# A state-space scan with experts on one core: GpSimd's waits, seven filler products, and GpSimd making each sixth drive product

## The chip, the core and the metric

The kernel runs on one core of a Trainium2 chip, in one launch. The time is the device time of that core in microseconds. TensorE (PE) multiplies matrices into PSUM; VectorE (DVE), ScalarE (ACT) and GpSimd (POOL) compute elementwise; SyncE (SP) issues most transfers. Each engine executes its own instructions in their order and waits on semaphores.

## The reference, cut to what matters

```
tokens = concat of three Hilbert patch embeddings of x, fused; with txt: 4 sequences of 384 tokens, 192 channels
xz = x @ in_proj_w.T;  x_branch, z = split(xz)
u  = silu(causal_conv4(x_branch));  dt = softplus(u @ dt_w.T + dt_b)
Bv = u @ B_w.T;  Cv = u @ C_w.T
for each of 16 states s, along the tokens t:
    h[t] = exp(dt[t] * A[s]) * h[t-1] + dt[t] * Bv[t, s] * u[t]      # decay * state + drive
    y[t] += h[t] * Cv[t, s]
y = ((y + D * u) * silu(z)) @ out_w.T;  then add and layer norm
router: top 2 of 8 experts per token;  expert = gelu(x @ Wi.T) @ Wo.T;  weighted sum
```

## The kernel before, in words

The tokens are cut into three chunks of 128. Channels lie on the partitions: four sequences of 128 channels and the 64 other channels of two pairs of them make six segments of 128 tokens, so a tile of the scan is 128 x 768, and 128 x 780 with two lead columns for each segment (one that clears the state, one that brings in the carry of the chunk before). The scan phase is one loop of 48 steps, `at` = 16 n + s: chunk n and state s. Each engine has this loop written out, with its own order.

In a step TensorE spreads the row of B over the partitions into a PSUM tile (`spread_b`, L815 to L818; two tiles, `wide(0)` and `wide(1)`, by turns). VectorE multiplies it in place with dt times u (the drive product, L1496), and then scans, with the decay from SBUF and the drive from PSUM (L1501), into one of two `states` tiles. ScalarE makes the decays ahead (`decay_of`, three SBUF tiles, L1225 and L1226) and brings in carries (`bring_carry`, L1233). GpSimd copies the last column of each segment as the carry for the next chunk (L574, steps 0 to 31) and multiplies the state with the row of C (L579) into one of two tiles. TensorE adds these up in PSUM (`sum_states`, L834 and L836), two steps behind. SyncE stores the rows of C to memory (`store_c`) and broadcasts one for each step (`broadcast_c`, L490 to L493, three transfers, a ring of three tiles), and from step 16 loads pieces of the experts' weights between them. VectorE waits before a scan for GpSimd's product of two steps ago.

Other work is inserted between the steps. On VectorE, after the scans of steps 3 and 4 the statistics and the normalisation of the last run of tokens (L1383, into `xn`), after 7 its convolution (L1422, L1426), after 11 the split of B in three bf16 parts (L1435 to L1444), after 13 softplus (L1454 to L1460). In the second and third chunk, after s = 1 the output product of the chunk before (L1505), after s = 7 the residual (L1513), after s = 8 the new rows of h (L1522), after s = 10 the router's rows (L1383, into `xf`), after s = 15 the two largest. GpSimd adds a shift to h (L566) before its waits of steps 1, 5 and 9. TensorE and ScalarE have their parts at other steps. Filler products keep TensorE busy in some places (`keep_warm` L773, `filler` L893).

Before the scan the patches are gathered by GpSimd's transfers (L552), transposed on TensorE (`patch_transposes`, L654), embedded (L660) and fused (L680); ScalarE copies between these. After the scan come the routing, and the loop over 31 tiles of expert rows.

## Time and profile before

| what | us |
|---|---|
| median of 3 runs | 461.56 (461.09 to 464.18) |
| the profiled execution | 460.29 |
| its span in the profile | 458.5 |
| VectorE's first scan starts | 74.2 |
| VectorE's last scan starts | 247.9 |
| mean granted clock of TensorE | 0.905 of 2.4 GHz |

The profile shows one execution. Its time is 1.8 us more than the span, which goes from the first to the last instruction; the median of the runs lies 1.3 us above the profiled execution. A row of the timeline has the start, the duration, the engine, the line, the output and the inputs, how many instructions are merged, and in brackets the idle time before them with what ended it. A float32 matmul shows as two records.

### The profile page before, as it was taken

Reading aid. Unit: us, or ns where it says so; the run is one execution under the profiler, and the core shown is the slowest. Engines: PE = TensorE matmul, PEld = TensorE weight load, DVE = VectorE, ACT = ScalarE, POOL = GpSimd, SP = SyncE. Lnnn points to the kernel's source line nnn. Section 1 sums busy time; section 2 is a strip of 40 time slices with the busy share of each in tenths; the row PEclk is TensorE's granted clock in tenths of the full one; section 3 lists DMA queues with packets and bytes.
Section 4 is the critical chain, followed back from the end, with each engine's and each line's share of the span. In section 5 each row is a group of like instructions: output and inputs, shape, how many; then the busy total and the mean of one; then the engine's idle time right before and its main releaser. Section 6 shows DMA issues by size and latency. Waiting matters only on the chain.

```text
span 458.5 us, 6697 instructions
## 1 busy us (share of the span) xinstructions
PE 383.5 (84%) x2283; PEld 285.0 (62%) x2283; DVE 294.9 (64%) x478; ACT 193.4 (42%) x459; POOL 224.9 (49%) x195
## 2 busy tenths in 40 slices
PE   5896997788758977879678875989999999999980
PEld 4453754454334643536344663979999999999970
DVE  4524379999999999999998638444343434344410
ACT  1555476637714465434642021024444444444430
POOL 6778723644526643656245003145656565656431
PEclk9997898979967996999779959599999999999996
DMA  6200012432424644766554730322323323333323
GB/s 183 60 9 4 7 31 92 125 92 59 127 70 150 172 155 115 214 188 190 133 144 114 310 113 38 104 59 43 48 54 46 54 44 56 47 53 46 43 27 112
DMA packets 33383, 42.76 MB, mean 93 GB/s; under 512 B 8302, under 2 KB 23391, under 8 KB 32783
## 3 DMA queue, kind: packets, MB, share of 16 engines
q1 hardware_dynamic: 26030, 34.76, 25.8%
q0 software_dynamic: 7328, 7.71, 10.9%
q8 instruction: 12, 0.20, 0.2%
q14 instruction: 13, 0.10, 0.1%
HBM read 36.55 MB, written 7.08 MB: 95 GB/s over the span
## 4 chain that ended last, share of the span: by engine, by line
PE 46%; issue 18%; POOL 17%; DVE 12%; DMA 3%; ACT 2%; POOLq 0%; SPq 0%; DVEq 0%; ACTq 0%
PE ps L1020 14%; PE ps L1003 9%; POOL w_all L579 9%; POOL w_all L552 6%; PE ps L1009 6%; DVE w_all L1501 4%; PE ps L834 3%; PE ps L979 2%; DVE ps L1496 2%; PE ps L773 2%; PE ps L993 2%; PE ps L836 1%; DVE y_cm L1426 1%; POOL carry L574 1%; DVE y_cm L1454 1%
## 5 line engine op out<-in xcount | busy, mean ns | idle before, releaser
L579 POOL TENSOR_TENSOR w_all<-w_all 128x768 f32<-128x768 f32 x48 | 81.3, 1693 | 29.4 <-DVE w_all L1501 24.1
L1501 DVE TENSOR_TENSOR_SCAN w_all<-decay,ps 128x780 f32<-128x780 f32 x48 | 85.4, 1779 | 1.6
L610 POOL DMA_INDIRECT sum_dram<-u_cm,tok_row x31 | 50.2, 1618 | 60.8 <-ACT u_cm L1329 58.2
L834 PE MATMUL ps<-w_all,cst 128*128 128x512 f32 x96 | 60.5, 716 | 7.8 <-POOL w_all L579 7.5
L552 POOL DMA_INDIRECT w_all<-in_pix,gidx x42 | 45.1, 1073 | 14.9 <-issue 12.5
L1314 ACT ACTIVATE u_cm<-ps,x_cm 128x128 f32<-128x128 f32 x96 | 26.5, 376 | 54.5 <-PE ps L1009 54.5
L1496 DVE TENSOR_TENSOR ps<-dtu_cm,ps 128x768 f32<-128x768 f32 x48 | 45.5, 947 | 1.2 <-PE ps L818 0.6
L574 POOL COPY carry<-w_all 128x6 f32<-128x6 f32 x32 | 6.7, 209 | 69.7 <-DVE w_all L1501 69.7
L1225 ACT ACTIVATE decay<-dt_cm,a_neg 128x512 f32<-128x512 f32 x48 | 34.2, 712 | 15.4 <-DVE dt_cm L1458 9.8
L595 POOL DMA_INDIRECT dt_cm<-x_dram,tok_in x31 | 31.2, 1005 | 19.3 <-DVE gate_s L1666 10.1
L773 PE MATMUL ps<-cst 128*128 128x256 f32 x114 | 34.5, 461 | 5.2 <-DMA cst<-in_cst 5.2
L1679 DVE COPY x_cm<-w_all 128x1154 f32 x16 | 12.2, 762 | 40.0 <-PE ps L1020 40.0
L836 PEld LDWEIGHTS ps<-w_all,cst 128*128 128x128 f32 x96 | 20.6, 215 | 27.8 <-issue 27.8
L1314 ACT ACTIVATE z_cm<-ps,y_cm 128x128 f32<-128x128 f32 x90 | 24.8, 375 | 27.0 <-PE ps L1009 27.0
L1020 PE MATMUL ps<-x_cm,u_cm 128*128 128x192 f32 x192 | 35.5, 333 | 0.0
L1679 DVE COPY y_cm<-w_all 128x1154 f32 x15 | 11.5, 766 | 35.9 <-PE ps L1020 35.9
L773 PEld LDWEIGHTS ps<-cst 128*128 128x128 f32 x114 | 26.0, 237 | 12.2 <-DMA cst<-in_cst 5.2
L1020 PE MATMUL ps<-y_cm,z_cm 128*128 128x192 f32 x180 | 33.4, 334 | 0.0
L815 PE MATMUL ps<-b_parts,pick 128*128 128x256 bf16 x48 | 14.0, 291 | 21.9 <-DVE w_all L1501 21.9
L1020 PEld LDWEIGHTS ps<-x_cm,u_cm 128*128 128x128 f32 x192 | 31.0, 189 | 1.8
L836 PE MATMUL ps<-w_all,cst 128*128 128x256 f32 x96 | 31.3, 411 | 0.0
L834 PEld LDWEIGHTS ps<-w_all,cst 128*128 128x128 f32 x96 | 17.7, 213 | 20.2 <-POOL w_all L579 15.8
(222 smaller groups left out, 722.5 us busy)
## 6 DMA issues: line engine op xcount, KB each, us to landing
w_all<-c_dram SPq DMA_DIRECT2D x48, 256.0 KB, 3.4
w_all<-c_dram SPq DMA_DIRECT2D x96, 64.0 KB, 3.5
w_all<-in_w_all SPq DMA_DIRECT2D x16, 289.0 KB, 3.9
w_all<-in_w_all SPq DMA_DIRECT2D x4, 1156.0 KB, 6.3
x_dram<-x_cm SPq DMA_DIRECT2D x3, 384.0 KB, 3.7
sum_dram<-h_tok SPq DMA_DIRECT2D x3, 384.0 KB, 3.9
out<-sum_dram SPq DMA_DIRECT2D x4, 288.0 KB, 3.6
w_all<-in_pix,gidx POOLq DMA_INDIRECT x42, 2.4
```

What stands on the lines that cost most here:

```text
L552: pool.indirect_dma_start(dst, None, d[table], bass.IndirectOffsetOnAxis(ap=gidx[:, col:col + 1].bitcast(U32), axis=0)).then_inc(signal, 16)
L579: nc.gpsimd.tensor_tensor(segments(hcs[at % 2]), inner(states[at % 2]), segments(c_sb[at % RING]), ALU.mult).then_inc(hc_rdy, 1)
L610: pool.indirect_dma_start(sum_dram, bass.IndirectOffsetOnAxis(ap=tok_row[:, i:i + 1].bitcast(U32), axis=0), y_out[:, i % 2, :], None, comp ...
L773: nc.tensor.matmul(ps[:, bank, 0:256], ident, cst[:, 0:256], start=True, stop=True)
L834: nc.tensor.matmul(sums[:, 0:4 * P], ident, hcs[at % 2][:, 0:4 * P], start=False, stop=at % S == S - 1, skip_group_check=True)
L836: nc.tensor.matmul(sums[:, 4 * P:6 * P], ident, hcs[at % 2][:, 4 * P:6 * P], start=False, stop=at % S == S - 1, skip_group_check=True).the ...
L1003: nc.tensor.matmul(ps[:, 2 + 2 * p + f // 3, P * (f % 3):P * (f % 3) + P], w[:, W_UA + P * f:W_UA + P * f + P], xe[:, p, 0:P], start=(f % ...
L1020: mm = nc.tensor.matmul(ps[:, 6 + p, 0:C], hid[p][:, P * f:P * f + P], w_now[p][:, W_DN + C * f:W_DN + C * f + C], start=(f == 0), stop=(f ...
L1225: nc.scalar.activation(o[:, 0:NB, :], chunk(dt3, n)[:, 0:NB, :], ACT.Exp, scale=a_neg[:, 0, s:s + 1])
L1314: ins = nc.scalar.activation(hid[p][:, P * f:P * f + P], ps[:, 2 + 2 * p + f // 3, P * (f % 3):P * (f % 3) + P], ACT.Gelu, bias=w_now[p][: ...
L1496: v.tensor_tensor(inner(wide(p)), chunk(dtu3, n), inner(wide(p)), ALU.mult).then_inc(driven, 1)
L1501: v.tensor_tensor_scan(states[p], decay[:, at % RING, :], wide(p), 0.0, ALU.mult, ALU.add).then_inc(scanned, 1)
```

## The change

It has three parts.

- GpSimd waits, before its product of steps 4, 7, 11, 13 (first chunk) and s = 8 and 10 (other chunks), until the work inserted on VectorE after that scan is done (`inserted_work`).
- TensorE makes seven more filler products ahead of the first patch transposes.
- GpSimd makes the drive product of the steps 5, 11, 17, ..., 47, three steps ahead, from a row of B that SyncE broadcasts into a new SBUF tile `b_wide_sb`. It writes the drive into the third decay tile, and ScalarE writes the decay of these steps into the PSUM tile that the drive would have had. TensorE spreads no B in these steps. The rows of B are stored to memory beside those of C. The carry copies go from GpSimd to ScalarE (`save_carry`), and VectorE's scan waits for them. After such a step ScalarE clears the carry's column where the tiles have changed roles.

```
...
+        b_wide_sb = sb("b_wide_sb", [P, 6 * P])
...
-        WARM = {"input weights": 10, "coarse levels": 2, "fine patches": 4, "normed rows": 7, "convolution": 2,
+        WARM = {"input weights": 10, "coarse levels": 2, "fine patches": 4, "patches": 7, "normed rows": 7, "convolution": 2,
...
+
+        def by_pool(at):
+
+            return at % 6 == 5
+
+        def pool_drives(at):
+            return (at + 1) // 6
+
+        def vector_drives(at):
+            return at + 1 - pool_drives(at)
...
-            def store_c(n):
+            def store_bc(n):
...
-                                     packed(bc_rows, n, 2)[64 * half + 3 * S:64 * half + 4 * S, :, a - lo:b - lo])\
-                            .then_inc(c_stored, 16)
+                                     packed(bc_rows, n, 2)[64 * half + 2 * S:64 * half + 4 * S, :, a - lo:b - lo])\
+                            .then_inc(bc_stored, 16)
+
...
             def broadcast_c(at):
 
                 r = at % RING
                 if at >= RING:
                     sp.wait_ge(hc_rdy, at - RING + 1)
-                sp.dma_start(c_sb[r][:, 0:4 * P], c_dram[at:at + 1, :].to_broadcast([P, 4 * P])).then_inc(c_ready[r], 16)
-                for half in range(2):
-                    sp.dma_start(c_sb[r][64 * half:64 * half + 64, 4 * P:6 * P],
-                                 c_dram[at:at + 1, 2 * P * half:2 * P * half + 2 * P].to_broadcast([64, 2 * P]))\
-                        .then_inc(c_ready[r], 16)
+                broadcast_row(c_sb[r], 2 * S * (at // S) + S + at % S, c_ready[r])
+
+            def broadcast_b(at):
+
+                if at >= 6:
+                    sp.wait_ge(pool_driven, pool_drives(at - 6))
+                broadcast_row(b_wide_sb, 2 * S * (at // S) + at % S, b_ready)
...
             for at in range(RING):
                 broadcast_c(at)
+            broadcast_b(5)
             piece = 0
             for at in range(RING, STEPS):
                 if at == S - 3:
-                    store_c(2)
-                if at == S:
-                    sp.wait_ge(c_stored, 16 * 8)
+                    store_bc(2)
                 broadcast_c(at)
+                if at == S - 2:
+                    sp.wait_ge(bc_stored, 16 * 8)
+                if by_pool(at - RING) and at - RING + 6 < STEPS:
+                    broadcast_b(at - RING + 6)
...
+            def inserted_work(n, s):
+
+                if n == 0:
+                    if s == 4:
+                        pool.wait_ge(xn_ready, 3)
+                    elif s == 7:
+                        pool.wait_ge(conv_step, 8 * 3)
+                    elif s == 11:
+                        pool.wait_ge(split_step, 5 * 3)
+                    elif s == 13:
+                        pool.wait_ge(dtu_rdy, 3)
+                elif s == 8:
+                    pool.wait_ge(h_new, n)
+                elif s == 10:
+                    pool.wait_ge(xf_rdy, n)
+
+            def pool_drive(at):
+
+                n = at // S
+                pool.wait_ge(dtu_rdy, min(n + 2, 3))
+                pool.wait_ge(b_ready, 48 * pool_drives(at))
+                pool.wait_ge(scanned, at - RING + 1)
+                nc.gpsimd.tensor_tensor(inner(decay[:, RING - 1, :]), chunk(dtu3, n), segments(b_wide_sb), ALU.mult)\
+                    .then_inc(pool_driven, 1)
+
             for at in range(STEPS):
                 if at in (1, 5, 9):
                     add_shift(at // 4)
                 pool.wait_ge(scanned, at + 1)
-                if at < STEPS - S:
-                    nc.gpsimd.tensor_copy(carry[:, at % S, :].rearrange("p (q o) -> p q o", o=1),
-                                          segments(states[at % 2])[:, :, SEG - 1:SEG]).then_inc(carry_saved, 1)
+                inserted_work(at // S, at % S)
                 pool.wait_ge(c_ready[at % RING], 48 * (at // RING + 1))
                 if at >= 2:
                     pool.wait_ge(summed, at - 1)
                 nc.gpsimd.tensor_tensor(segments(hcs[at % 2]), inner(states[at % 2]), segments(c_sb[at % RING]),
                                         ALU.mult).then_inc(hc_rdy, 1)
+                if by_pool(at + RING):
+                    pool_drive(at + RING)
...
             coarse_rows()
             keep_warm(WARM["fine patches"], 0)
             interpolated(0)
+            keep_warm(WARM["patches"], 7)
             patch_transposes(0)
             keep_warm(1, 7)
             fine_level(0)
...
             def spread_b(at):
 
                 n, s, p = at // S, at % S, at % 2
+                if by_pool(at):
+                    return
                 if at >= 2:
                     pe.wait_ge(scanned, at - 1)
                 else:
...
             def decay_of(at):
                 n, s = at // S, at % S
-                if s == 0:
+                if s == 0 or s == 1:
                     act.wait_ge(dt_rdy, min(n + 2, 3))
-                if at >= RING:
-                    act.wait_ge(scanned, at - RING + 1)
-                o = inner(decay[:, at % RING, :])
+                if by_pool(at):
+                    act.wait_ge(scanned, at - 1)
+                    o = inner(wide(at % 2))
+                    if n:
+                        lead = segments(wide(at % 2))
+                        nc.scalar.activation(lead[:, :, 1:2], lead[:, :, 0:1], ACT.Copy)
+                else:
+                    if at >= RING:
+                        act.wait_ge(scanned, at - RING + 1)
+                    o = inner(decay[:, at % RING, :])
+                    if n and by_pool(at - RING):
+                        lead = segments(decay[:, at % RING, :])
+                        nc.scalar.activation(lead[:, :, 1:2], lead[:, :, 0:1], ACT.Copy)
                 nc.scalar.activation(o[:, 0:NB, :], chunk(dt3, n)[:, 0:NB, :], ACT.Exp, scale=a_neg[:, 0, s:s + 1])
                 nc.scalar.activation(o[:, NB:6, :], chunk(dt3, n)[:, NB:6, :], ACT.Exp, scale=a_neg[:, 1, s:s + 1])\
                     .then_inc(decay_rdy, 1)
 
+            def save_carry(at):
+                act.wait_ge(scanned, at + 1)
+                nc.scalar.activation(carry[:, at % S, :].rearrange("p (q o) -> p q o", o=1),
+                                     segments(states[at % 2])[:, :, SEG - 1:SEG], ACT.Copy).then_inc(carry_saved, 1)
+
             def bring_carry(at):
 
                 act.wait_ge(carry_saved, at - S + 1)
-                act.wait_ge(b_wide, at + 1)
-                nc.scalar.activation(segments(wide(at % 2))[:, :, 1:2],
+                if by_pool(at):
+                    act.wait_ge(scanned, at - RING + 1)
+                    lead = segments(decay[:, RING - 1, :])
+                else:
+                    act.wait_ge(b_wide, vector_drives(at))
+                    lead = segments(wide(at % 2))
+                nc.scalar.activation(lead[:, :, 1:2],
                                      carry[:, at % S, :].rearrange("p (q o) -> p q o", o=1), ACT.Copy).then_inc(carry_set, 1)
...
             patches_transposed(1)
             for at in range(STEPS):
                 n, s = at // S, at % S
+                if by_pool(at + 1):
+                    decay_of(at + 1)
+                if 0 <= at - 1 < STEPS - S:
+                    save_carry(at - 1)
                 if S <= at + 1 < STEPS:
                     bring_carry(at + 1)
-                if at + 2 < STEPS:
+                if at + 2 < STEPS and not by_pool(at + 2):
                     decay_of(at + 2)
                 if n == 0:
                     if s == 0:
...
                 n, p = at // S, at % 2
                 if at % S == 0:
                     dve.wait_ge(dtu_rdy, min(n + 2, 3))
-                dve.wait_ge(b_wide, at + 1)
                 if n:
                     dve.wait_ge(carry_set, at - S + 1)
-                v.tensor_tensor(inner(wide(p)), chunk(dtu3, n), inner(wide(p)), ALU.mult).then_inc(driven, 1)
-                dve.wait_ge(driven, at + 1)
+                if by_pool(at):
+                    dve.wait_ge(pool_driven, pool_drives(at))
+                    fade, drive = wide(p), decay[:, RING - 1, :]
+                else:
+                    dve.wait_ge(b_wide, vector_drives(at))
+                    v.tensor_tensor(inner(wide(p)), chunk(dtu3, n), inner(wide(p)), ALU.mult).then_inc(driven, 1)
+                    dve.wait_ge(driven, vector_drives(at))
+                    fade, drive = decay[:, at % RING, :], wide(p)
                 dve.wait_ge(decay_rdy, at + 1)
                 if at >= 2:
                     dve.wait_ge(hc_rdy, at - 1)
-                v.tensor_tensor_scan(states[p], decay[:, at % RING, :], wide(p), 0.0, ALU.mult, ALU.add).then_inc(scanned, 1)
+                    if at - 2 < STEPS - S:
+                        dve.wait_ge(carry_saved, at - 1)
+                v.tensor_tensor_scan(states[p], fade, drive, 0.0, ALU.mult, ALU.add).then_inc(scanned, 1)
```

The rows of C and B take the place of `c_dram` in `bc_dram`; semaphores and the waits on them are renamed accordingly.

GpSimd, first chunk, products of steps 2 to 4. Before:

```order
L574 COPY carry<-w_all 128x6 [waits scanned]
L579 TENSOR_TENSOR w_all<-w_all 128x768 [waits summed,c_ready2]
L574 COPY carry<-w_all 128x6 [waits scanned]
L579 TENSOR_TENSOR w_all<-w_all 128x768 [waits summed,c_ready0]
L574 COPY carry<-w_all 128x6 [waits scanned]
L579 TENSOR_TENSOR w_all<-w_all 128x768 [waits summed,c_ready1]
L566 TENSOR_TENSOR h_tok<-h_tok,ln_gb 128x768 [waits xn_ready]
```

Now:

```order
L627 TENSOR_TENSOR w_all<-w_all 128x768 [waits summed,c_ready2,scanned]
L616 TENSOR_TENSOR decay<-dtu_cm,b_wide_sb 128x6x128 [waits scanned,b_ready,dtu_ready]
L627 TENSOR_TENSOR w_all<-w_all 128x768 [waits summed,c_ready0,scanned]
L627 TENSOR_TENSOR w_all<-w_all 128x768 [waits c_ready1,summed,xn_ready,scanned]
L591 TENSOR_TENSOR h_tok<-h_tok,ln_gb 128x768 [waits xn_ready]
```

The carry copies are gone, the drive for step 5 stands behind the product of step 2, and the product of step 4 waits for the normalised rows.

VectorE, steps 16 to 18. Before:

```order
L1496 TENSOR_TENSOR ps<-dtu_cm,ps 128x6x128 [waits carry_set,b_wide,dtu_ready]
L1501 SCALAR_TENSOR_TENSOR w_all<-decay,ps 128x780 [waits hc_rdy,decay_rdy,driven]
L1496 TENSOR_TENSOR ps<-dtu_cm,ps 128x6x128 [waits carry_set,b_wide]
L1501 SCALAR_TENSOR_TENSOR w_all<-decay,ps 128x780 [waits hc_rdy,decay_rdy,driven]
L1505 TENSOR_TENSOR y_cm<-ps,z_cm 128x6x128 [waits summed]
L1496 TENSOR_TENSOR ps<-dtu_cm,ps 128x6x128 [waits carry_set,b_wide]
```

Now:

```order
L1577 TENSOR_TENSOR ps<-dtu_cm,ps 128x6x128 [waits b_wide,carry_set,dtu_ready]
L1585 SCALAR_TENSOR_TENSOR w_all<-decay,ps 128x780 [waits hc_rdy,carry_saved,decay_rdy,driven]
L1585 SCALAR_TENSOR_TENSOR w_all<-ps,decay 128x780 [waits hc_rdy,decay_rdy,carry_saved,pool_driven,carry_set]
L1589 TENSOR_TENSOR y_cm<-ps,z_cm 128x6x128 [waits summed]
L1577 TENSOR_TENSOR ps<-dtu_cm,ps 128x6x128 [waits b_wide,carry_set]
```

The product of step 17 is gone, and its scan has the inputs the other way round.

## Rows read from the trace of the kernel before

**Rows 1.** The page's costliest groups: busy us, mean ns | idle before, its releaser.
```profile
L1501 DVE TENSOR_TENSOR_SCAN w_all<-decay,ps 128x780 f32<-128x780 f32 x48 | 85.4, 1779 | 1.6
...
L574 POOL COPY carry<-w_all 128x6 f32<-128x6 f32 x32 | 6.7, 209 | 69.7 <-DVE w_all L1501 69.7
```

**Rows 2.** VectorE's timeline in a plain step: start us, duration us, line, instruction.
```profile
152.10 0.94 DVE L1496 TENSOR_TENSOR ps<-dtu_cm,ps 128x768 f32<-128x768 f32 x1
...
153.07 1.78 DVE L1501 TENSOR_TENSOR_SCAN w_all<-decay,ps 128x780 f32<-128x780 f32 x1
...
154.77 0.94 DVE L1496 TENSOR_TENSOR ps<-dtu_cm,ps 128x768 f32<-128x768 f32 x1
```

**Rows 3.** GpSimd's timeline.
```profile
90.72 1.81 POOL L566 TENSOR_TENSOR h_tok<-h_tok,ln_gb 128x768 f32<-128x768 f32 x1
...
163.08 1.68 POOL L579 TENSOR_TENSOR w_all<-w_all 128x768 f32<-128x768 f32 x1
```

**Rows 4.** VectorE's timeline outside the scan.
```profile
50.56 1.32 DVE L1383 TENSOR_SCALAR xn<-h_tok,mv,rstd 128x192 f32<-128x192 f32 x4 [0.28 <-DVE rstd L1379]
...
56.81 2.33 DVE L1426 SCALAR_TENSOR_TENSOR y_cm<-x_cm,chan,y_cm 128x512 f32<-128x512 f32 x3
...
64.62 0.48 DVE L1437 SCALAR_TENSOR_TENSOR w_all<-b_parts,cst,w_all 128x256 f32<-128x256 bf16 x1
...
68.05 3.08 DVE L1454 SCALAR_TENSOR_TENSOR y_cm<-w_all,y_cm 128x768 f32<-128x768 f32 x3
...
260.60 1.40 DVE L1522 SCALAR_TENSOR_TENSOR h_tok<-w_all,rstd,h_tok 128x192 f32<-128x192 f32 x4
```

**Rows 5.** VectorE's timeline, the inserted work of the scan.
```profile
88.86 4.09 DVE L1383 TENSOR_SCALAR xn<-h_tok,mv,rstd 128x192 f32<-128x192 f32 x4
...
102.32 3.67 DVE L1426 SCALAR_TENSOR_TENSOR y_cm<-x_cm,chan,y_cm 128x524 f32<-128x524 f32 x3
...
118.76 1.96 DVE L1437 SCALAR_TENSOR_TENSOR w_all<-b_parts,cst,w_all 128x262 f32<-128x262 bf16 x1
...
128.25 4.58 DVE L1454 SCALAR_TENSOR_TENSOR y_cm<-w_all,y_cm 128x786 f32<-128x786 f32 x3
...
168.67 2.83 DVE L1522 SCALAR_TENSOR_TENSOR h_tok<-w_all,rstd,h_tok 128x192 f32<-128x192 f32 x4
...
178.67 2.62 DVE L1383 TENSOR_SCALAR x_cm<-h_tok,mv,rstd 128x192 f32<-128x192 f32 x4
```

**Rows 6.** One window: us; busy PE, PEld, DVE, ACT, POOL; clock; DMA share, GB/s.
```profile
40.50:48.00 7.50, 7.48 (x19) 4.74 (x20) 2.91 (x4) 4.09 (x7) 5.98 (x6) 0.50 0.07 4
```

**Rows 7.** TensorE's timeline, the patch chain.
```profile
40.52 1.05 PE L654 MATMUL ps<-cst,w_all 128*48 128x128 f32 x4 [3.68 <-ACT w_all L1073]
...
42.35 1.97 PE L660 MATMUL ps<-w_all 48*64 48x512 f32 x2
...
45.26 2.77 PE L680 MATMUL ps<-w_all 65*128 65x192 f32 x8
```

**Rows 8.** TensorE's timeline at either clock: sum of states, then B's spreading.
```profile
139.49 2.08 PE L834 MATMUL ps<-w_all,cst 128*128 128x512 f32 x2 [0.23 <-POOL w_all L579]
...
142.21 0.40 PE L815 MATMUL ps<-b_parts,pick 128*128 128x256 bf16 x1
...
157.53 1.13 PE L834 MATMUL ps<-w_all,cst 128*128 128x512 f32 x2
...
158.49 0.59 PE L836 MATMUL ps<-w_all,cst 128*128 128x256 f32 x2
...
158.92 0.27 PE L815 MATMUL ps<-b_parts,pick 128*128 128x256 bf16 x1
```

**Rows 9.** Rows of C: issues with us to landing (page), and SyncE's timeline.
```profile
w_all<-c_dram SPq DMA_DIRECT2D x96, 64.0 KB, 3.5
...
162.48 1.08 SPq L493 DMA_DIRECT2D w_all<-c_dram  x2
```

**Rows 10.** VectorE's timeline beside GpSimd's product at 163.08.
```profile
164.36 1.39 DVE L1513 SCALAR_TENSOR_TENSOR w_all<-ps,mv,ln_gb 128x192 f32<-128x192 f32 x4
```

More of the change, by code:

```diff
@@ L319, in build @@
         bc_copied = sem("bc_copied")
-        c_stored = sem("c_stored")
+        bc_stored = sem("bc_stored")
         split_step = sem("split_step")
@@ L337, in build @@
         driven = sem("driven")
+        b_ready = sem("b_ready")
+        pool_driven = sem("pool_driven")
         scanned = sem("scanned")
@@ L480, in store_c, with broadcast_row @@
                     for half in range(2):
-                        sp.dma_start(c_dram.rearrange("(j s) (b t) -> j s b t", j=NJ, b=NB)
+                        sp.dma_start(bc_dram.rearrange("(j s) (b t) -> j s b t", j=NJ, b=NB)
                                      [j, :, 2 * half:2 * half + 2, a - P * j:b - P * j],
-                                     packed(bc_rows, n, 2)[64 * half + 3 * S:64 * half + 4 * S, :, a - lo:b - lo])\
-                            .then_inc(c_stored, 16)
+                                     packed(bc_rows, n, 2)[64 * half + 2 * S:64 * half + 4 * S, :, a - lo:b - lo])\
+                            .then_inc(bc_stored, 16)
+            def broadcast_row(dst, row, signal):
+                sp.dma_start(dst[:, 0:4 * P], bc_dram[row:row + 1, :].to_broadcast([P, 4 * P])).then_inc(signal, 16)
+                for half in range(2):
+                    sp.dma_start(dst[64 * half:64 * half + 64, 4 * P:6 * P],
+                                 bc_dram[row:row + 1, 2 * P * half:2 * P * half + 2 * P].to_broadcast([64, 2 * P]))\
+                        .then_inc(signal, 16)
             def broadcast_c(at):
@@ L506, in send_rows @@
                                  xf[:, NB * j:NB * j + NB, src:C]).then_inc(x_sent, 16)
-            store_c(0)
-            store_c(1)
-            sp.wait_ge(c_stored, 16 * 4)
+            store_bc(0)
+            store_bc(1)
+            sp.wait_ge(bc_stored, 16 * 4)
             for at in range(RING):
                 broadcast_c(at)
+            broadcast_b(5)
             piece = 0
```

4 lines of the change are left out of this document (2 added, 2 removed).

## The prediction

> **What bounds the kernel now.** I read the page first. Its busy shares are averages over stages and name no bound; its costliest groups do [rows 1]: before its 48 scans VectorE was idle for 1.6 us in total, so from 74.2 to 249.7 us, where the scan steps run, VectorE is the bound. From 299 us on TensorE runs the expert tiles back to back, as the chain of waits tells, and the change touches nothing there. In a plain step its product starts at 152.10, its scan at 153.07, its next product 1.70 later [rows 2]: a period of 2.67 us, of which 0.97 is the product. GpSimd's product takes 1.68 us of that [rows 3], and then it waits for the next scan.
>
> The second thing to see is that some VectorE instructions inserted between steps are far longer than the same work elsewhere. Before and after the scan, when GpSimd has no elementwise work, they take the times of [rows 4]; inside it those of [rows 5]. Each long one overlaps a GpSimd product: the four normalisations at 88.86 take 4.09 us instead of 1.32, and GpSimd's addition of the shift ends at 92.53, 0.4 us before them [rows 3]. They read both operands from SBUF, or write SBUF from SBUF. The scan and its product, with one operand in PSUM, keep 1.78 and 0.94 us beside GpSimd.
>
> The third: TensorE idles 3.68 us before 40.52 and then runs its patch chain at a granted clock of 0.50, which is 1.2 GHz, from 40.5 to 48 [rows 6, 7].
>
> **The warming products.** They fill 36.84 to 40.52, an idle gap on TensorE. From 40.52 three pieces of its work stand on the path, each waited for by ScalarE and then VectorE: 1.05, 1.97 and 2.77 us at 1.2 GHz. That level costs twice the other: the same sum of states takes 2.72 us from its start to the next matmul at 1.2 GHz and 1.39 at 2.4 [rows 8]. So 5.79 us become 2.9: **2.9 us gained**. Seven products at 2.4 GHz take 7 x 0.43 = 3.0 us, which nearly fills the gap; 0.43 is the distance from 158.49 to 158.92, a matmul of the same shape [rows 8]. Lower bound of the gain: nothing, if the clock falls anyway. What is late next is VectorE's chain from 48.06, which simply starts sooner; the seven products behind it halve too and stay under cover.
>
> **GpSimd's waits.** Six places, priced by [rows 5] minus [rows 4], scaled to 131 columns instead of 128 where needed: normalisation of the input 4.09 - 1.32 = 2.77; convolution 3.67 - 2.38 = 1.29; splitting B 1.96 - 0.49 = 1.47; softplus 4.58 - 3.15 = 1.43; new rows of h 2.83 - 1.40 = 1.43, twice; router's rows 2.62 - 1.32 = 1.30, twice. **12.4 us gained.** The wait delays GpSimd's product of that step to the end of the inserted work. Behind it on GpSimd stand the next products, and VectorE's scan two steps on waits for it; that scan starts 0.97 + 1.70 + 0.97 = 3.6 us later, and the product takes 1.68, so nothing appears there. Two exceptions below.
>
> **The eight drive products.** VectorE drops eight of 0.97 us: **7.8 us gained**. GpSimd adds eight of 1.68 us in slots where it is idle: with its six products and one drive it has 11.8 us of work in 15.1. It makes the drive three steps ahead, right after its product of step D-3. Taking the end of scan D-3 as 0: product 0.05 to 1.75, drive to 3.45, product D-2 to 5.2 instead of 4.4, while scan D may start at 5.35. It fits, by 0.15 us. The 32 carry copies (6.7 us in all on GpSimd [rows 1]) go to ScalarE; their cover is its idle time in every step, and if that went, each would cost 0.2 us. The decay that goes to PSUM is the same two activations; a small copy that clears the carry's place comes to 11 of them, beside the same idle time. The eight extra broadcasts cost SP some 1.5 us each, as each of C's does (1.08 for its last two pieces, after the first). A C broadcast has 5.4 us or more from its release to its use, and needs 0.9 to issue its last piece and 3.5 for it to land [rows 9]. The rows of B double the size of eight small stores to memory, which nobody waits for while VectorE is held. Their second wait moves from step 16 to 14 on SP; the store was issued a step before, and behind it stands only the row for step 15, used two steps later.
>
> **What comes back.**
> - GpSimd, step 8: the delayed product 7, product 8, drive 11 and the addition of the shift (1.8 us, as at 90.72 [rows 3]) queue before product 9. Scan 11 waits for that: 1.6 us (0 to 1.8).
> - TensorE's order: behind the late product D-2 stand its sum (1.4) and only then the spreading of B for step D+1 (some 0.5), and from step 16 on the carry on ScalarE (0.2 and the signals). That ends at 7.6 or so where VectorE wants it at 7.15. Where inserted work follows (D = 5, 11, 17, 23, 41) it is covered; at D = 29 and 35 I put 0.3 and 0.7. Bounds 0 and 8 x 0.7.
> - ScalarE: the decay of step 5 goes before its table load at 85.67, and the decay of step 29 behind the router's copies: 0.3 + 0.5.
> - Softplus into the second chunk: product 13 now starts only after softplus, so TensorE idles some 6 us and then sums at 1.2 GHz (2.72 each); the first output product needs three sums in a row. 1.5 us (0 to 3).
> Together 4.9.
>
> **A page's rule against it.** The four instructions at 164.36 [rows 10] have their first operand in PSUM and their second in SBUF; the first of them runs beside a GpSimd product that ends at 164.76 [rows 3], and the four take 1.39 us. Four of the same size with GpSimd idle take 1.40 [rows 4]. So I take the new scans, decay from PSUM and drive from SBUF, at 1.78. The Trainium skill, page "SBUF — State Buffer", section "Who interferes with whom", says that a VectorE instruction with two SBUF inputs contends with GpSimd's reads because its second input comes through the shared read interface. Read for the second input alone, that would make the eight new scans and GpSimd block each other, and the sum 451 (the first rival); the same section also says that an instruction with at most one SBUF input does not contend, which is what this row shows.
>
> **Sum.** 2.9 + 12.4 + 7.8 = 23.1 us gained, 4.9 given back: 18.2. The profiled execution took 460.29 us (span 458.5): 442.1. The median of the runs, 461.56, stands 1.27 above it, so **443.4 us**. Its own range is 440 (little given back) to 447 (clock and order at their bounds).
>
> **Rivals.**
> - *The shared operand path (0.10).* The new scans and GpSimd's products exclude each other. Scan D starts at 5.35, product D-1 would start at 5.41 and now at 7.15; scan D+1 waits 0.3 us more, the spreading for D+2 some 0.6. About 1 us a step: 8 us, 451. For: the instructions of [rows 5]. Against: [rows 10].
> - *The waits only move the stall (0.07).* The late products surface in later scans: 443.4 + 12.4 = 455.8. Against: 3.6 us of room for 1.68.
> - *The warming does not hold the clock (0.10).* 446.3. For: the clock fell inside an idle gap; against: the gap is filled.
> - *SP's queue (0.05).* B's broadcasts push C's: up to 8 x 1.5 = 12 us, 455.4. For: C's rows already take 4.4 of the 5.4 us that a shorter step leaves [rows 9]. Against: B's broadcast stands behind C's of the same step, and the next row of C has a step more.
> - *TensorE becomes the bound at 1.2 GHz (0.03), slower than before.* A step there takes it 2.72 (sum) + 0.86 (filler, twice 0.43) + 0.4 (spreading, the row at 142.21 alone) = 4.0 us [rows 8], 1.3 more than the period. The waits and the eight missing spreadings lengthen its idle times, and if the low level held for more than 18.2 / 1.3 = 14 steps beyond now, the change would lose; over 30 such steps it is 443.4 + 39 = 482. For: the row at 139.49 is at 1.2 GHz, behind the pause for softplus. Against: the clock was back at 157.53, and the waits shorten the inserted work that makes the pauses.
>
> The forecast gets 0.65. The range 439.5 to 451 takes in the forecast, the first and the third rival (0.85) and leaves out the other three. A measurement of this kernel tells about 1% (4.6 us) from no change. All cases but the last are faster by more than that: faster 0.95, within 1% 0.02 (several of them together), slower 0.03.
>
> **What the profile after would show.** A granted clock of 1.0 from 40.5 to 48 and the first scan near 71.3 instead of 74.2. Normalisations, convolution, split, softplus and new rows at the times of [rows 4]. Eight scans reading PSUM first at 1.78 us, each 1.70 after the scan before. The last scan near 229.9 + 1.8 instead of 247.9 + 1.8, then the same 209 us to the end. Scan 11 about 1.6 us late behind GpSimd. I am wrong if those eight scans are longer, if VectorE waits for GpSimd or TensorE for more than some 6 us in the scan, or if TensorE's low clock spreads.

## The result and the profile after

The change made the kernel faster: 445.88 us median of 4 runs (445.39 to 449.09) beside 461.47 of before (461.09 to 464.18), a ratio of 0.9687 [0.9644, 0.9729]. The profiled execution took 445.39 us, its span is 443.6 against 458.5.

VectorE in the changed kernel, chosen rows of its timeline: start, duration, line, what it does, and in brackets how long VectorE sat idle before and for whom. Here L1585 is the scan, L1577 its product, L1589 the output product; the others are inserted work.

```profile
72.02 1.78 DVE L1585 TENSOR_TENSOR_SCAN w_all<-decay,ps 128x780 f32<-128x780 f32 x1
80.79 0.96 DVE L1577 TENSOR_TENSOR ps<-dtu_cm,ps 128x768 f32<-128x768 f32 x1 [1.65 <-PE ps L871]
87.92 1.25 DVE L1460 TENSOR_SCALAR xn<-h_tok,mv,rstd 128x192 f32<-128x192 f32 x4
...
96.80 2.36 DVE L1503 SCALAR_TENSOR_TENSOR y_cm<-x_cm,chan,y_cm 128x524 f32<-128x524 f32 x3
110.83 1.78 DVE L1585 TENSOR_TENSOR_SCAN w_all<-ps,decay 128x780 f32<-128x780 f32 x1 [1.79 <-POOL w_all L627]
112.84 0.49 DVE L1514 SCALAR_TENSOR_TENSOR w_all<-b_parts,cst,w_all 128x262 f32<-128x262 bf16 x1
120.86 3.14 DVE L1531 SCALAR_TENSOR_TENSOR y_cm<-w_all,y_cm 128x786 f32<-128x786 f32 x3
158.05 1.41 DVE L1606 SCALAR_TENSOR_TENSOR h_tok<-w_all,rstd,h_tok 128x192 f32<-128x192 f32 x4
166.63 1.25 DVE L1460 TENSOR_SCALAR x_cm<-h_tok,mv,rstd 128x192 f32<-128x192 f32 x4
194.46 0.96 DVE L1577 TENSOR_TENSOR ps<-dtu_cm,ps 128x768 f32<-128x768 f32 x1 [2.17 <-ACT ps L1306]
230.54 1.78 DVE L1585 TENSOR_TENSOR_SCAN w_all<-ps,decay 128x780 f32<-128x780 f32 x1
238.22 0.96 DVE L1589 TENSOR_TENSOR y_cm<-ps,z_cm 128x768 f32<-128x768 f32 x1 [4.96 <-PE ps L889]
```

Every inserted instruction that took 1.96 to 4.58 us in [rows 5] now takes about its time of [rows 4]: 1.25 for 4.09, 2.36 for 3.67, 0.49 for 1.96, 3.14 for 4.58, 1.41 for 2.83, 1.25 for 2.62. Three waits stand out: at 110.83, at 194.46, and the last output product, 7.68 us behind the last scan where it was 5.18.

The groups by line and shape show the moved work. The eight scans whose first operand is in PSUM keep their 1.77 us; GpSimd's drive product takes 1.81 us and its product of the state 1.68 (busy time in us and mean ns of one; then the idle time before them and what ended it):

```profile
L1585 DVE TENSOR_TENSOR_SCAN w_all<-ps,decay 128x780 f32<-128x780 f32 x8 | 14.2, 1774 | 2.0 <-POOL w_all L627 1.8
L616 POOL TENSOR_TENSOR decay<-dtu_cm,b_wide_sb 128x768 f32<-128x768 f32 x8 | 14.5, 1812 | 0.0
L627 POOL TENSOR_TENSOR w_all<-w_all 128x768 f32<-128x768 f32 x48 | 80.5, 1681 | 75.2 <-DVE w_all L1585 32.2 <-DVE h_tok L1606 10.4 <-DVE dtu_cm L1537 7.2
L1577 DVE TENSOR_TENSOR ps<-dtu_cm,ps 128x768 f32<-128x768 f32 x40 | 37.9, 948 | 4.6 <-ACT ps L1306 2.8 <-PE ps L871 1.6
```

The warmed stretch, in the columns of [rows 6] (stretch, its length, busy time and count of TensorE, its weight loads, VectorE, ScalarE and GpSimd, granted clock, DMA share, GB/s):

```profile
40.50:48.00 7.50, 6.46 (x30) 4.54 (x30) 4.50 (x13) 5.73 (x11) 5.98 (x6) 1.00 0.06 6
```

The clock is 1.00 instead of 0.50. The span therefore divides like this, both profiles cut at the same instructions:

| stretch | before | after | difference | predicted |
|---|---|---|---|---|
| to the first scan | 74.16 | 72.02 | -2.14 | -2.9 |
| first to last scan | 173.78 | 158.52 | -15.26 | -15.3 |
| last scan to last output product | 5.18 | 7.68 | +2.50 | 0 |
| from there to the end | 205.4 | 205.4 | 0 | 0 |
| span | 458.5 | 443.6 | -14.9 | -18.2 |

### The profile page after: what moved, and what is told of

The parts are those of the page before. It is cut to its first block, busy times and chain, and to the rows that moved or that the text cites. A ratio compares the mean times of both kernels' runs of the same rounds, so it can differ in the third digit from the quotient of the medians.

```text
span 443.6 us, 6744 instructions
## 1 busy us (share of the span) xinstructions
PE 373.6 (84%) x2265; PEld 280.8 (63%) x2265; DVE 274.4 (62%) x470; ACT 197.9 (45%) x502; POOL 233.7 (53%) x171
## 4 chain that ended last, share of the span: by engine, by line
PE 40%; DVE 20%; issue 14%; POOL 12%; DMA 4%; SPq 4%; ACT 2%; POOLq 0%; DVEq 0%; ACTq 0%
PE ps L1073 15%; PE ps L1056 9%; DVE w_all L1585 7%; POOL w_all L577 6%; PE ps L1062 6%; DVE ps L1577 4%; POOL w_all L627 4%; PE ps L1032 2%; SPq L502 2%; DVE y_cm L1531 2%; DVE y_cm L1503 2%; PE ps L1046 2%; PE ps L887 1%; DVE stats L1440 1%; DMA b_wide_sb<-bc_dram 1%
## 5 line engine op out<-in xcount | busy, mean ns | idle before, releaser
L887 PE MATMUL ps<-w_all,cst 128*128 128x512 f32 x96 | 57.3, 681 | 21.8 <-POOL w_all L627 21.6
L1585 DVE TENSOR_TENSOR_SCAN w_all<-decay,ps 128x780 f32<-128x780 f32 x40 | 71.1, 1779 | 1.5 <-POOL w_all L627 0.2
L1577 DVE TENSOR_TENSOR ps<-dtu_cm,ps 128x768 f32<-128x768 f32 x40 | 37.9, 948 | 4.6 <-ACT ps L1306 2.8
L887 PEld LDWEIGHTS ps<-w_all,cst 128*128 128x128 f32 x96 | 17.2, 205 | 33.5 <-POOL w_all L627 29.1
L889 PEld LDWEIGHTS ps<-w_all,cst 128*128 128x128 f32 x96 | 19.8, 206 | 25.9 <-issue 25.9
L823 PEld LDWEIGHTS ps<-cst 128*128 128x128 f32 x128 | 26.9, 218 | 11.5 <-DMA cst<-in_cst 5.3
L1763 DVE COPY y_cm<-w_all 128x1154 f32 x15 | 11.4, 762 | 36.0 <-PE ps L1073 36.0
L1288 ACT ACTIVATE decay<-dt_cm,a_neg 128x512 f32<-128x512 f32 x40 | 28.5, 712 | 7.6 <-DVE dt_cm L1535 7.4
L1073 PEld LDWEIGHTS ps<-y_cm,z_cm 128*128 128x128 f32 x180 | 29.0, 189 | 1.8
L1056 PE MATMUL ps<-u_cm,x_cm 128*128 128x128 f32 x192 | 24.1, 275 | 0.0
```

What stands on the lines that cost most here:

```text
L823: nc.tensor.matmul(ps[:, bank, 0:256], ident, cst[:, 0:256], start=True, stop=True)
L887: nc.tensor.matmul(sums[:, 0:4 * P], ident, hcs[at % 2][:, 0:4 * P], start=False, stop=at % S == S - 1, skip_group_check=True)
L889: nc.tensor.matmul(sums[:, 4 * P:6 * P], ident, hcs[at % 2][:, 4 * P:6 * P], start=False, stop=at % S == S - 1, skip_group_check=True).the ...
L1056: nc.tensor.matmul(ps[:, 2 + 2 * p + f // 3, P * (f % 3):P * (f % 3) + P], w[:, W_UA + P * f:W_UA + P * f + P], xe[:, p, 0:P], start=(f % ...
L1073: mm = nc.tensor.matmul(ps[:, 6 + p, 0:C], hid[p][:, P * f:P * f + P], w_now[p][:, W_DN + C * f:W_DN + C * f + C], start=(f == 0), stop=(f ...
L1577: v.tensor_tensor(inner(wide(p)), chunk(dtu3, n), inner(wide(p)), ALU.mult).then_inc(driven, 1)
```

## The experiments

Each run below carries a profile too, and the profile is the finer tool: most steps of the scan repeat to some hundredths of a microsecond, so a wait can be seen at its place. The runs were made in three sets, each with the kernel before beside it: the first four kernels below "before, again", the next four, and the last three with "before, again". In the first two sets the kernel before took 494 and 496 us, not 461, and each of the eight variants in them reached its first scan near 109 us. Most of the loss lies ahead of the scan, and the kernel before has it too (the last section shows it), so those sets are read by the ratio to the kernel before, run beside them, and by stretches behind the first scan.

| kernel | median us (before beside it) | ratio [95%] | first to last scan | last scan to output product |
|---|---|---|---|---|
| before, again | 460.66 (461.46) | 0.9987 [0.9954, 1.002] | 174.78 | 5.19 |
| warming alone | 501.05 (494.32) | 1.0141 [1.0091, 1.0191] | 176.87 | 5.19 |
| waits alone | 484.57 (494.32) | 0.9806 [0.9757, 0.9855] | 163.39 | 5.19 |
| warming and waits | 485.6 (494.32) | 0.9829 [0.9761, 0.9896] | 163.06 | 5.64 |
| the change without waits | 496.42 (494.32) | 1.0039 [1.0013, 1.0065] | 173.07 | 6.03 |
| the change again | 483.41 (495.79) | 0.9822 [0.9763, 0.9882] | 157.04 | 7.25 |
| with filler products | 485.39 (495.79) | 0.9825 [0.9762, 0.9889] | 158.69 | 11.76 |
| SP's queue reordered | 480.57 (495.79) | 0.9746 [0.9681, 0.9811] | 157.20 | 6.02 |
| shift at step 22 | 481.91 (495.79) | 0.9716 [0.9637, 0.9796] | 160.89 | 7.38 |
| decay in SBUF | 453.53 (461.46) | 0.9848 [0.9795, 0.9901] | 163.31 | 7.47 |
| queue, shift at 17 | 444.62 (461.46) | 0.965 [0.9599, 0.9701] | 160.27 | 6.03 |
| queue, shift at 17, filler | 442.69 (461.46) | 0.9595 [0.955, 0.9641] | 158.11 | 6.02 |

### GpSimd's waits, alone and left out

The kernel before with the six waits only:

```diff
+                inserted_work(at // S, at % S)
                 pool.wait_ge(c_ready[at % RING], 48 * (at // RING + 1))
```

> The kernel before with GpSimd's six kinds of waits alone. If the long inserted instructions are long only because GpSimd reads SBUF beside them, they fall to the times of rows 4 and the time by 12.4 us less what queues behind the late product 7: 461.5 - 11.5 = 450. If the waits only move the stall to the next scans: 461.5.

And the change with that one line taken out again, so that the drives stand alone (beside the warming):

> The changed kernel without GpSimd's waits. If they are worth as much beside the drives as alone: 445.9 + 12 = 458. If GpSimd's extra drive products lengthen the overlap with the inserted work: more than that, 460 and over. If the drives' gain covers the loss of the waits: under 452.

VectorE with the waits alone, then without them beside the drives:

```profile
123.66 1.25 DVE L1400 TENSOR_SCALAR xn<-h_tok,mv,rstd 128x192 f32<-128x192 f32 x4
156.54 3.14 DVE L1471 SCALAR_TENSOR_TENSOR y_cm<-w_all,y_cm 128x786 f32<-128x786 f32 x3
```

```profile
124.17 4.13 DVE L1459 TENSOR_SCALAR xn<-h_tok,mv,rstd 128x192 f32<-128x192 f32 x4
152.93 1.78 DVE L1584 TENSOR_TENSOR_SCAN w_all<-ps,decay 128x780 f32<-128x780 f32 x1 [1.80 <-ACT decay L1288]
164.30 4.42 DVE L1530 SCALAR_TENSOR_TENSOR y_cm<-w_all,y_cm 128x786 f32<-128x786 f32 x3
...
212.49 4.12 DVE L1459 TENSOR_SCALAR x_cm<-h_tok,mv,rstd 128x192 f32<-128x192 f32 x4
```

The waits decide whether inserted work is long. Alone they shorten the scan by 10.4 us against the first profile of before and by 11.4 against its second. With the waits left out the change is no faster than before (1.0039). A part of that is the warming's loss in this set, shown below: beside the warming alone the drives still gain 4.6 us (501.05 to 496.42), 3.8 of them in the scan (176.87 to 173.07), half of their 7.8. With the waits back the scan is 14.6 to 16.0 us shorter (158.52 and 157.04 us), more than the waits bring alone, which is the second case of the expectation: the router's rows at 212.49 take 4.12 us beside GpSimd's product and the drive behind it, where they took 2.61 with the warming alone, beside a product only. The second fence holds a surprise too: scan 11 waits 1.80 us although GpSimd waits for no inserted work, and the wait is put down to ScalarE.

### The warming products, alone and with the waits

```diff
             interpolated(0)
+            keep_warm(WARM["patches"], 7)
             patch_transposes(0)
```

> The kernel before with the seven filler products alone. If the patch chain at 1.2 GHz was what they cure: first scan some 2.1 to 2.9 us earlier than 74.2, the clock 1.0 from 41 to 48 us, time 461.5 - 2.5 = 459. If the clock gain comes back later (the scan phase is paced by VectorE and does not care when it starts, so it should not): 461.5.

> The kernel before with the filler products and the waits, without the drive products on GpSimd. If the parts add up: 461.5 - 2.5 - 11.5 = 447.5, and the drives were worth only 1.6 us of their 7.8. If the queue on GpSimd behind product 7 (1.8 us) and the late rows of C at the end (2.5 us) come with the drives: the same 447.5. If they come with the waits: 450 or more, and the drives were worth 4.

Neither pair can measure the gain, since the stretch they act in was the disturbed one. There the seven products gained nothing, and alone they lost: the first scan came at 109.73 and 110.50 us with them and at 107.80 with the waits alone, and warming alone took 501.05 us beside 494.32. Its scan stretch, 176.87 us, is longer than either of before by 2.1 us or more; 0.8 of that is a wait at step 36, behind products of TensorE at 1.2 GHz. Why the rest came is open. What speaks for a gain are the undisturbed profiles: before twice, 74.16 and 74.32 us to the first scan, with a clock of 0.50 from 44 to 48 us, in the patch chain; the four warmed kernels, 72.02, 71.75, 71.29 and 73.53, with 1.00 there. So 0.6 to 3.0 us, over 2 in three of the four, and at 73.53 the clock fell a little later, between 48 and 56 us (0.79). These four hold the drives and the waits too; the warming alone was not measured undisturbed, so that the gain is its own is argued from the clock at its place and not shown by a run. Step 3 is another place: it is 1.2 us late where TensorE drops to 1.2 GHz early enough ahead of it, in one of two profiles of before and in three of these four. Whether the warming has a part in that, these runs do not tell.

### The drives, seen against warming and waits

> The changed kernel once more, as the base for the three beside it: 445.5 to 446.

Warming and waits together need 163.06 us from first to last scan, the change 158.52 and 157.04: 4.5 to 6.0 us for the eight drives of 7.8. The two profiles of the change differ at one place, step 36. TensorE there, first in the second profile and then in the first:

```profile
225.31 1.12 PE L880 MATMUL ps<-u_cm,diag 128*128 128x512 f32 x2 [2.39 <-DVE y_cm L1589]
226.70 1.02 PE L887 MATMUL ps<-w_all,cst 128*128 128x512 f32 x2
227.99 1.02 PE L887 MATMUL ps<-w_all,cst 128*128 128x512 f32 x2
```

```profile
188.00 1.13 PE L880 MATMUL ps<-u_cm,diag 128*128 128x512 f32 x2 [3.01 <-DVE y_cm L1589]
189.56 1.92 PE L887 MATMUL ps<-w_all,cst 128*128 128x512 f32 x2
192.12 1.27 PE L887 MATMUL ps<-w_all,cst 128*128 128x512 f32 x2
```

Behind a pause that VectorE's output product ends (there is no spreading of B to do for a step that GpSimd drives), the two sums run at 2.4 GHz in one and, from 189, at 1.2 GHz in the other; the carry copy and the product of step 36 wait for what stands behind them, 2.17 us in the slow case and 0.48 in the other. The low clock there is not the drives' alone: with the waits only, where B is spread at this place, the first of these sums took 1.85 us and the product of step 36 waited 1.24. Most of the rest of the missing gain is scan 11, in both.

### Filler in that pause

```diff
                     elif s not in (2, 4):
                         filler()
+                    elif n == 2 and s == 2:
+                        pe.wait_ge(logit_rdy, 1)
+                        keep_warm(6, 5)
```

> The changed kernel with six filler products (128x256) on TensorE at step 34, in the pause of 3.0 us before the skip term of the third chunk. If the 2.17 us that VectorE waits before the product of step 36 come from the clock that falls in this pause: that wait falls to 0.7 or less and the time by 1.4, to 444.4. If they come from the order of TensorE's work alone: the fillers change nothing, 445.9.

> As after_two, with six filler products on TensorE in its pause of 3 us behind step 34, which wait for the router's copies. Theory: the sums of steps 34 and 35 then run at 2.4 GHz, and the product of step 36 waits 0.6 us instead of 2.2; first to last scan 155.2 us where after_two shows the low clock there, the same where it doesn't. Rival (the clock there falls or not by itself, as it stayed up in one of the change's two profiles): no systematic difference between the two.

With the filler the sums at that place took 1.02 us in both runs, and the step from scan 35 to scan 36 took 3.2 us, where the first profile of the change, the reordered queue and the shift at 22 show 4.7 to 4.9 (its second profile 3.2, without filler). That is no proof yet. In the kernel with the decay in SBUF, also without filler, TensorE paused 3.02 us at this place and its sums took 1.02 all the same. Of the seven profiles with drives and without filler two kept the high clock, of the two with filler both, so the rival, that it falls or not by itself, is not excluded. The cleanest pair is the last: in the kernel without the filler, then in the one with it, VectorE and TensorE show

```profile
191.41 1.66 PE L888 MATMUL ps<-w_all,cst 128*128 128x512 f32 x2
195.43 0.96 DVE L1578 TENSOR_TENSOR ps<-dtu_cm,ps 128x768 f32<-128x768 f32 x1 [2.17 <-ACT ps L1307]
```

```profile
187.54 2.76 PE L824 MATMUL ps<-cst 128*128 128x256 f32 x12
192.11 1.02 PE L888 MATMUL ps<-w_all,cst 128*128 128x512 f32 x2
195.49 0.96 DVE L1581 TENSOR_TENSOR ps<-dtu_cm,ps 128x768 f32<-128x768 f32 x1 [0.48 <-ACT ps L1310]
```

The wait is 1.7 us shorter, at its place. In its first run the filler brought no gain in time (485.39 us beside the change's 483.41): there a row of C reached GpSimd 3.08 us late behind the last scan, TensorE paused another 3.19 us, and its sums at 272.81 took 2.08 us. That is the next experiment's subject.

### SP's queue at the end

The last output product comes later than before in each kernel that has drives, by 0.84 us or more, and by 0.45 in the one with warming and waits. Behind the last scan of the change GpSimd waits for a row of C. SP's queue and GpSimd there, rows of two views; for SP the duration is that of issuing:

```profile
222.10 2.34 SPq L502 DMA_DIRECT2D w_all<-bc_dram  x2
224.49 1.14 SPq L527 DMA_DIRECT2D x_dram<-x_cm  x2
225.67 0.73 SPq L522 DMA_DIRECT2D w_all<-in_w_all  x1
226.44 0.45 SPq L500 DMA_DIRECT2D w_all<-bc_dram  x1
226.94 1.09 SPq L502 DMA_DIRECT2D w_all<-bc_dram  x2
...
232.32 3.31 POOL L627 TENSOR_TENSOR w_all<-w_all 128x768 f32<-128x768 f32 x2 [1.91 <-DVE w_all L1585]
```

The profile names the last scan, which ends at 232.32 too. But the first of the two products in this row needs only the scan before, and in the change's second profile it began 0.43 us ahead of the last scan's end. What is left is its row of C, issued at 226.44 behind two stores of the router's rows and an expert's weights. I moved both behind the last row of C:

```diff
-                if at > S and at % S == 13:
+                if at == 2 * S - 3:
...
-                if at >= S and at % 2 and piece < PIECES * (E - LATE):
+                if S <= at < 2 * S + 12 and at % 2 and piece < PIECES * (E - LATE):
...
+            send_rows(1)
```

> The changed kernel with the two stores of router's rows and the last two pieces of expert weights issued behind the last row of C instead of before it. If GpSimd's product 46 at 232.32 came late because its row of C stood behind them in SP's queue: it starts as its scan ends, the output product follows the last scan after 5.2 us instead of 7.7, and the time falls by up to 2.5, to 443.4. If it was late for another reason: 445.9. If the stores and weights are then late themselves: slower than 445.9.

```profile
267.68 3.41 POOL L628 TENSOR_TENSOR w_all<-w_all 128x768 f32<-128x768 f32 x2 [0.26 <-DVE w_all L1586]
273.57 0.96 DVE L1590 TENSOR_TENSOR y_cm<-ps,z_cm 128x768 f32<-128x768 f32 x1 [3.30 <-PE ps L890]
```

GpSimd's wait is 0.26 us and the output product stands 6.02 us behind the last scan, in all three kernels with the reordered queue (6.02, 6.03, 6.02) against 7.25 to 11.76 with the old order and the waits. So the issue order cost 1.2 to 1.7 us. But the stores and weights stood in the same place in the kernel before, where SP issued that row as soon as it was released. Two kernels that were run for another question tell what made the difference. GpSimd near the last scan, first with warming and waits but no drives (the last scan starts at 273.56), then with drives but no waits (281.34):

```profile
273.30 1.67 POOL L596 TENSOR_TENSOR w_all<-w_all 128x768 f32<-128x768 f32 x1 [1.54 <-DMA w_all<-c_dram]
```

```profile
281.46 3.42 POOL L626 TENSOR_TENSOR w_all<-w_all 128x768 f32<-128x768 f32 x2 [0.26 <-DVE w_all L1584]
```

The row is late without any broadcast of B, and in time with all eight of them, so the waits on GpSimd are what it takes. SP issues the row for step 45 when the product of step 42 is done, and the row for step 46 when that of step 43 is. The wait for the router's rows delays product 42: the two ends lie 5.4 us apart in before and 2.6 with the waits. Into that time go the row for step 45 (1.4 to 2.7 us of issuing), the stores (1.1 to 1.6) and the weights (0.7 to 0.9). The row for step 46 is then issued 0.9 to 1.0 us late with the waits and no drives, and 1.4 and 2.1 in the change's two profiles. The extra there is longer issues at this place (2.34 us for two transfers in the rows above, 1.09 elsewhere); whether B's broadcasts cause them was not tested. Only in the first run with filler is a broadcast of B itself in the way: one of its issues took 2.69 us.

What is left over 5.18 stays: the last scan is a GpSimd-driven one, 0.94 us closer to the scan before it. GpSimd's product of step 46 and TensorE's sum of it begin 0.93 us further back behind the last scan, the residual's products and the last sum stand behind that sum, and the output product comes 0.84 us later.

### The third addition of the shift

```diff
-                if at in (1, 5, 9):
-                    add_shift(at // 4)
+                if at in (1, 5, 22):
+                    add_shift(min(at // 4, 2))
```

> The changed kernel with GpSimd's third addition of the shift at step 22 instead of 9. If the queue behind product 7 is what holds scan 11: the wait of 1.79 us before scan 11 goes and the time falls by 1.8, to 444.1. If TensorE or ScalarE are as late there: less than 1.

Scan 11 and ScalarE with the addition out of the way:

```profile
148.69 1.78 DVE L1585 TENSOR_TENSOR_SCAN w_all<-ps,decay 128x780 f32<-128x780 f32 x1 [1.25 <-ACT carry L1294]
```

```profile
146.04 1.28 ACT L1288 ACT_TABLE_LOAD   x1
147.34 0.69 ACT L1288 ACTIVATE ps<-dt_cm,a_neg 128x512 f32<-128x512 f32 x1
147.97 0.46 ACT L1289 ACTIVATE ps<-dt_cm,a_neg 128x256 f32<-128x256 f32 x1
```

The wait fell from 1.79 only to 1.25 us. GpSimd was the last to be ready in the change, but ScalarE is ready only half a microsecond before it: the decay of step 11 stands behind two copies of softplus's input, which wait 2.40 us for TensorE, and a table load of 1.28 (the carry copy that the wait names comes right behind that decay). At step 22 the addition has its own price: the rows of h at step 24 wait 0.76 us more. At step 17 it costs less there:

> The change with two edits: the last writing of rows to memory on SP is issued behind the last broadcasts of C (as in after_spq), and GpSimd's third addition of the shift is made at step 17 instead of 9. Theory: the queue edit takes the last scan to the routing scan from 31.2 or 31.6 us to 28.5 again; the addition at step 17 takes scan 11's wait from 1.8 to 1.25 us, what ScalarE's table load leaves (its decay of step 11 is ready then), and costs nothing at step 24, unlike at step 22, where it cost 0.9. So first to last scan 0.5 us shorter than after_spq (157.2): 156.7, and 480.0 us beside after_spq's 480.6. Rival (GpSimd's queue at steps 17 to 20 has no room either): the 0.5 us comes back at step 20 or 24.

Scan 11 waits 1.25 us there too, in both kernels; of the 0.54 us gained, the next step gives 0.25 back. The scan stretch is 160.27 where 156.7 was expected, and longer than the 157.20 of the queue edit alone: by 1.25 us in step 3, where TensorE fell to 1.2 GHz, by 1.0 in step 7, where VectorE waits 1.06 us for TensorE, by 0.6 in step 8, and smaller ones. In the kernel with the filler, scan 23 waits 1.42 us for GpSimd, whose product waits 1.33 us for a row of C. That did not happen with the addition at step 9 in the change's two profiles; whether the addition at step 17 brings it is not tested. With the filler it is the fastest kernel of all, 0.9595 [0.955, 0.9641]; the change itself has 0.9687 [0.9644, 0.9729], measured apart, so their order is likely but not shown by one set of runs.

### The decay in SBUF

```diff
-                    o = inner(wide(at % 2))
+                    o = inner(fade_sb)
...
-                    fade, drive = wide(p), decay[:, RING - 1, :]
+                    fade, drive = fade_sb[:, :], decay[:, RING - 1, :]
```

> The change, but the decay of the eight steps whose drive GpSimd makes lies in a tile in SBUF instead of PSUM, so that these scans read both operands from SBUF. Theory (one operand in PSUM is what keeps VectorE clear of GpSimd): the stretch from the first to the last scan start, 157.0 to 158.5 us in the change's two profiles, becomes up to 8 us longer (about 1 us for each such step), and these scans take more than 1.78 us, or GpSimd's products beside them more than 1.68. Rival (a scan with both operands in SBUF runs beside GpSimd's product as well, so that the place of the decay is indifferent): the stretch stays at 157 to 158.5 and the eight scans at 1.78.

Two rows of VectorE and two of GpSimd:

```profile
112.36 3.08 DVE L1584 TENSOR_TENSOR_SCAN w_all<-fade_sb,decay 128x780 f32<-128x780 f32 x1 [1.80 <-POOL w_all L628]
177.20 3.29 DVE L1584 TENSOR_TENSOR_SCAN w_all<-fade_sb,decay 128x780 f32<-128x780 f32 x1
```

```profile
87.84 3.04 POOL L628 TENSOR_TENSOR w_all<-w_all 128x768 f32<-128x768 f32 x1 [3.63 <-DVE xn L1459]
137.50 4.72 POOL L628 TENSOR_TENSOR w_all<-w_all 128x768 f32<-128x768 f32 x2 [0.80 <-DVE w_all L1584]
```

With both operands in SBUF a scan and a GpSimd product no longer run side by side: of the eight scans two take 3.08 and 3.29 us in place of 1.78, and beside five of the others GpSimd's product takes longer (3.04 in place of 1.68, or two of them 3.65 to 4.72 in place of 3.35). The stretch is 4.8 to 6.3 us longer than in the change's two profiles, and the kernel takes 453.53 us. So the first rival's mechanism exists, and PSUM is what kept the change clear of it.

### The kernel before once more

> The kernel before, unchanged, for a profile on the same chip as the others. All eight variants showed 36 us more ahead of the first scan than the first two profiles, with TensorE issuing one matmul in 1.4 to 2.8 us from 24 to 63 us. Theory (it belongs to the chip's condition, not to the change): the kernel before shows the same, its first scan at about 107.8 us (as with the waits alone, which act only later), and then 173.8 us to the last scan and 29.0 to the routing scan, as in its first profile. Rival (it comes from something in the variants): its first scan at 74 us and 461 us in all.

460.66 us, first scan at 74.32, 174.78 to the last scan: it repeats, and the third set of runs had none of the disturbance. So the expectation's first case did not come. It tells only in part where the lost 36 us belong: before's own profile in that condition was not taken, its time was (494 and 496 us).

## Why the prediction was right, and what it missed

It said 443.4 us and the median was 445.88, inside both ranges, in the main by the forecast's mechanism.

- **Warming, 2.9 us.** 2.14. The clock held and the chain's three pieces took 0.62, 1.07 and 1.57 us against 1.05, 1.97 and 2.77, 2.5 us less. But the chain began 0.66 us later than the 40.52 of [rows 7], a start that the step took for fixed. The traces show where that comes from: the chain waits for the gathered patches, and GpSimd's sixth gather took 3.88 us instead of 3.08. In the kernel with the decay in SBUF, warmed in the same way, it took 3.08, and the chain began at 40.68. So this is a difference from run to run.
- **Waits, 12.4 us.** The durations give 12.7; alone on the chip 10.4 to 11.4, since 1.3 us came back at step 36, where TensorE summed at 1.2 GHz. "So nothing appears there" was wrong at this place, and at the tail below.
- **Drives, 7.8 us.** 4.5 to 6.0 net within the scan, for the reasons under what came back. The decisive choice, the scan's 1.78 us with one operand in PSUM by [rows 10], was right. The Trainium skill's sentence that VectorE with two SBUF inputs contends with GpSimd's reads ("SBUF — State Buffer", "Who interferes with whom") agrees with the decay-in-SBUF run (scans of 3.08 and 3.29 us); the narrower reading, that the second input alone decides, does not agree with the eight scans at 1.77.
- **What came back in the scan, 4.9 us.** 5.2 (12.7 and 7.8, less the 15.26 that the stretch gained), but made up differently. Scan 11: 1.79 for 1.6, with ScalarE ready only half a microsecond before GpSimd, which I had missed. Step 30, behind D = 29: 0.24 for 0.3. Step 36, behind D = 35: 2.17 us for 0.7; the term for TensorE's order was worked out at 2.4 GHz, and TensorE was at 1.2 there; a wait of 1.24 stood there with the waits alone. Step 3: 1.2 us more of a wait for TensorE, which one of two profiles of before has too. Softplus's boundary showed 0.37 for 1.5, and ScalarE nothing for 0.8. That the sum comes within 0.3 us is luck: two terms too high cover one too low and one that was not there, and the second profile, with step 36 at the high clock, lies 1.5 us lower.
- **The last rows, none.** This is the step that failed: "the last scan, then the same 209 us to the end". It took 2.5 us more. A row of C that SP issues late, behind stores and weights, is 1.7 us of that by the reordered queue. It looks like the rival of SP's queue, but B's broadcasts are not what makes it: with them and without GpSimd's waits the row is in time. It is a second price of the waits, which bring SP's two releases closer together. 0.8 us is the shorter last step itself.

So the sum of 18.2 became 14.9: 0.8 less from the warming, 2.5 at the tail.

## What to carry to other kernels

When an engine's stalls come from another engine's use of SBUF, first let the other engine wait out the long pieces: without the waits the change's scan was 14.6 us longer or more, and the kernel no faster than before. In this kernel a scan with one operand in PSUM ran at its full speed beside GpSimd, and moving an operand to PSUM can be what makes sharing the work possible. Then ask what the delayed engine releases: here its late product let SP issue the next rows in a shorter time, with other transfers between them. Inside the loop most late rows were absorbed (in the change GpSimd waited 1.84 us for one at 178.72 and no scan did), one was not (1.42 us at scan 23 of the fastest kernel), and behind the last scan there is no later step to absorb one.

## What was unexpected of the hardware

In two sets of runs TensorE, from about 24 to 63 us, issued one matmul in 1.4 to 2.8 us for much of the time, with nothing in the profile that it waited for, while GpSimd was issuing its gathers at the usual 1.25 us each. The second profile of the change, this stretch and some matmuls in it:

```profile
24.00:63.00 39.00, 15.85 (x56) 8.08 (x56) 0.00 (x0) 2.01 (x4) 25.47 (x27) 0.53 0.07 5
```

```profile
53.38 0.57 PE L817 MATMUL ps<-u_cm,bc 64*64 64x250 f32 x1 [2.22 <-issue]
56.18 0.57 PE L817 MATMUL ps<-u_cm,bc 64*64 64x250 f32 x1 [2.23 <-issue]
58.98 0.57 PE L813 MATMUL ps<-u_cm,dw 128*64 128x250 f32 x1 [2.23 <-issue]
```

56 matmuls in 39 us, where the first profile of the change has 208 in the same stretch. All eight kernels of these sets had it (46 to 60 matmuls) and none of the third set. The three sets ran on three different chips, so something of the chip, or of what ran on it, is not excluded. Its cause stays open; no run tested it.

The second: GpSimd's product takes 1.81 us when it makes the drive and 1.68 when it multiplies the states, at the same 128 x 768 elements. Why is open.
